# Attention 1 of a two-attention kernel: scores one item ahead, output weights converted later, a new order at the passage to attention 2

## The reference

```python
# attention 1: 32 heads of 128, 8 key/value heads, ALiBi-like bias, causal
qkv = h @ w_qkv                                   # h: x times a gate
scores = einsum('bqhd,bkhd->bhgqk', q, k) * 128 ** -0.5
attn = softmax(scores - slopes * sqrt(distance))  # -inf above the diagonal
x = x + einsum('bhgqk,bkhd->bqhgd', attn, v).reshape(B, S, 4096) @ w_o
# attention 2: q and k RMS-normed and rotated; 512 cached keys and values from pages, then 128 own ones
scores = einsum('bqhd,bhkd->bhqk', q, k_all) / sqrt(128)
y = einsum('bhqk,bhkd->bhqd', softmax(masked scores), v_all) @ Wo.T
# then a LayerNorm and two 8-bit-quantised linear layers; x = x + result
```

## Time and profile before

| | us |
|---|---|
| median of three runs | 2095.12 (2093.95 to 2095.36) |
| the profiled execution | 2088.9 |
| its span, first to last instruction | 2087.1 |
| TensorE busy | 2011.7 |
| VectorE, ScalarE, GpSimd busy | 1534.5, 1331.6, 825.6 |
| mean granted TensorE clock | 0.988 of full |

### The profile page before, as it was taken

One profiled execution on the slowest core, in us unless ns is written; L12 is line 12 of the kernel. 1 busy time (PEld: TensorE's weight loads), 2 busy tenths in 40 slices (PEclk: granted clock), 3 DMA queues, 4 the chain that ended last, 5 costly groups with the idle time before them and its releaser, 6 DMA issues.

```text
span 2087.1 us, 35849 instructions
## 1 busy us (share of the span) xinstructions
PE 2011.7 (96%) x12456; PEld 1701.8 (82%) x12456; DVE 1534.5 (74%) x3381; ACT 1331.6 (64%) x3810; POOL 825.6 (40%) x812
## 2 busy tenths in 40 slices
PE   6999999999999999989999999999999999999985
PEld 5777777888888888868888888888888888888873
DVE  5677765556656555568887887888878878888887
ACT  3567773445544544457776776777767767777785
POOL 4100014100000000035666666666666666666773
PEclk9999999999999999999999999999999999999997
DMA  8011101101201110111121110111211111112000
GB/s 299 26 52 47 51 1 71 61 31 36 67 31 36 56 46 6 56 46 50 31 83 31 61 52 31 62 52 31 83 32 62 53 31 62 53 31 81 27 31 30
DMA packets 45010, 108.60 MB, mean 52 GB/s; under 512 B 15634, under 2 KB 21010, under 8 KB 40354
## 3 DMA queue, kind: packets, MB, share of 16 engines
q1 hardware_dynamic: 28450, 72.74, 10.1%
q0 software_dynamic: 16384, 33.59, 5.3%
HBM read 103.14 MB, written 3.15 MB: 51 GB/s over the span
## 4 chain that ended last, share of the span: by engine, by line
PE 87%; DVE 7%; ACT 4%; issue 1%; DMA 0%; POOLq 0%; POOL 0%; SPq 0%; DVEq 0%; ACTq 0%
PE PS L1640 10%; PE PS L1544 8%; PE PS L1652 8%; PE PS L1416 8%; PE PS L1472 7%; PE PS L1607 7%; PE PS L1625 6%; PE PS L1558 4%; PE PS L1429 4%; PE PS L1610 3%; PE PS L344 3%; PE PS L1459 2%; PE PS L1444 2%; PE PS L334 2%; PE PS L500 1%
## 5 line engine op out<-in xcount | busy, mean ns | idle before, releaser
L2453 POOL DMA_INDIRECT kcache<-in_kcache,rows x256 | 251.2, 981 | 545.2 <-DVE x_res L1789 474.6
L2461 POOL DMA_INDIRECT vcache<-in_vcache,rows x256 | 257.5, 1006 | 137.4 <-PE PS L1444 61.7
L1935 DVE CUSTOM_DVE_ANT_0 pr<-PS,ffn_weights,sm 128x640 f32<-128x640 f32 x256 | 225.4, 885 | 96.5 <-PE PS L1610 96.4
L1951 DVE TENSOR_TENSOR prT_lo<-PS,prT_hi 128x512 fp32r<-128x512 f32 x320 | 209.4, 686 | 36.0 <-ACT prT_hi L2316 23.6
L2305 ACT ACTIVATE pr<-pr,sm 128x640 f32<-128x640 f32 x256 | 212.5, 831 | 36.5 <-DVE sm L1935 36.1
L2316 ACT ACTIVATE prT_hi<-PS 128x512 fp32r<-128x512 f32 x320 | 178.6, 597 | 66.3 <-PE PS L1625 63.7
L1625 PE MATMUL PS<-consts,pr 128*128 128x128 f32 x1280 | 174.0, 273 | 3.3 <-issue 1.5
L1625 PEld LDWEIGHTS PS<-consts,pr 128*128 128x128 f32 x1280 | 149.7, 141 | 29.4 <-issue 3.2
L2467 POOL TENSOR_TENSOR vcached_lo<-vcache,vcached_hi 128x512 fp32r<-128x512 f32 x64 | 83.2, 1300 | 226.7 <-ACT vcached_hi L2288 226.7
L2180 ACT ACTIVATE pr<-pr,sm 128x128 f32<-128x128 f32 x256 | 99.7, 391 | 100.5 <-DVE sm L1779 100.5
L1607 PE MATMUL PS<-kT_lo,qT_hi 128*128 128x320 f32 x512 | 154.1, 309 | 0.0
(11 more groups left out here) (324 smaller groups left out, 6224.9 us busy)
## 6 DMA issues: line engine op xcount, KB each, us to landing
arena<-in_wqkv SPq DMA_DIRECT2D x16, 1536.0 KB, 6.5
arena<-in_wo SPq DMA_DIRECT2D x16, 1024.0 KB, 5.5
arena<-in_wcT SPq DMA_DIRECT2D x8, 1024.0 KB, 5.8
kcache<-in_kcache,rows POOLq DMA_INDIRECT x256
vcache<-in_vcache,rows POOLq DMA_INDIRECT x256
arena<-in_xT SPq DMA_DIRECT2D x8, 256.0 KB, 6.6
x_res<-in_x SPq DMA_DIRECT2D x1, 2048.0 KB, 14.8
ffn_weights<-in_alibi SPq DMA_DIRECT2D x2, 1024.0 KB, 7.1
```

Of the source, the lines that this page charges most:

```text
L1935: dve.tensor_tensor_reduce(pr2[:, h, :].rearrange("p (a n) -> p a n", a=2), PS[:, SCORE_BANK[h]:SCORE_BANK[h] + 2, 0:HALF], keymask[:, b, ...
L1951: dve.tensor_tensor(prT2[1][:, n % 3, :, :].rearrange("p h n -> p (h n)"), bank(4 + n % 2), prT2[0][:, n % 3, :, :].rearrange("p h n -> p ...
L2453: pool.indirect_dma_start(out=kcache[:, c, :], out_offset=None, in_=T["kcache"], in_offset=bass.IndirectOffsetOnAxis(ap=rows[:, g, b, c:c ...
L2461: pool.indirect_dma_start(out=vcache[:, c, :], out_offset=None, in_=T["vcache"], in_offset=bass.IndirectOffsetOnAxis(ap=rows[:, g, b, c:c ...
```

## The change

In the TensorE's `step1`, the scores of items from 7 on move from the head of their item to the item before, between `turn_probs1` and `weigh1`; `turn_k1` of the same item goes ahead of the first head part. The VectorE's `softmax_max1(i + 1)` goes to the end of its step i, ahead of the sum's low part. In a group's first item three of the four low parts of output weights go behind the sum's low part, and `project_out1` waits for each quarter of those weights instead of all. In items 59 to 63 the work for attention 2 is distributed in another way over the items on all engines. On the GpSimd `load_values(0)` is split in two.

```diff
+        AHEAD = range(7, ITEMS)
             def project_out1(i):
-                pe.wait_ge(a1_wol, GH * (i // B + 1))
...
                 for h in range(GH):
+                    if i % B == 0 or h == 0:
+                        pe.wait_ge(a1_wol, GH * (i // B) + h + 1 if i % B == 0 else GH * (i // B + 1))
...
             def step1(i):                      # TensorE
-                scores1(i)
+                if i not in AHEAD:
+                    scores1(i)
                 if i + 1 < ITEMS:
                     if i > GH:
                         project_kv1(i + 1)
                 else:
                     project_kv(0)
-                    turn_cached_k(0)
+                if i == ITEMS - 1:
+                    turn_q(0)
                 if i >= FROM_X:
                     turn_x(i - FROM_X)
                 project_out1(i - 1)
+                if i + 1 in AHEAD:
+                    turn_k1(i + 1)
...
-                elif i == ITEMS - 3:
-                    project_q(0, (0,))
                 turn_probs1(i)
-                if i + 1 < ITEMS:
+                if i + 1 in AHEAD:
+                    scores1(i + 1)
+                elif i + 1 < ITEMS:
                     turn_k1(i + 1)
...
+                elif i == ITEMS - 5:
+                    project_q(0, (0, 1))
+                elif i == ITEMS - 4:
+                    project_q(0, (2,))
                 elif i == ITEMS - 3:
-                    project_q(0, (1, 2))
+                    project_q(0, (3,))
                 elif i == ITEMS - 2:
-                    turn_q(0)
+                    turn_cached_k(0)
                 elif i == ITEMS - 1:
-                    turn_k(0)
+                    project_q(1, (0, 1, 2))
                 weigh1(i)
...
                 elif i == ITEMS - 1:
-                    project_q(1)
+                    turn_k(0)
+                    project_q(1, (3,))
...
             def step1(i):                      # VectorE
                 g, b = group_of(i)
-                softmax_max1(i)
+                if i not in AHEAD:
+                    softmax_max1(i)
...
+                if i == ITEMS - 5:
+                    lo_of_weights(0, 0)
+                    lo_of_weights(0, 1)
+                if i == ITEMS - 4:
+                    lo_of_weights(0, 2)
+                if i == ITEMS - 3:
+                    lo_of_weights(0, 3)
+                if i == ITEMS - 2:
+                    dve.wait_ge(s_rope, 1)
+                    spread_q(0)
+                normalise1(i)
+                if b == B - 2 and g < G - 1:
+                    lo_of_weights1(g + 1, GH)
                 if i >= FROM_X:
                     lo_of_x(i - FROM_X)
+                if i == ITEMS - 2:
+                    lo_of_weights(0, KT)
+                    lo_of_probs1(i)
+                    add1(i - 1)
                     lo_of_v1(i + 1)
+                    join_q(0)
+                elif i == ITEMS - 1:
+                    lo_of_cached_k(0)
+                    lo_of_own_v(0)
                     rotate_k(0)
+                    lo_of_probs1(i)
                     norm_k(0)
+                    add1(i - 1)
                     lo_of_q(0)
                     lo_of_own_k(0)
+                else:
+                    add1(i - 1)
+                    lo_of_v1(i + 1)
+                    lo_of_probs1(i)
                 if b < GH and 0 < g < G - 1:
                     lo_of_weights1(g + 1, b)
+                if i + 1 == ITEMS - 1:
+                    add_alibi1(i + 1)
+                    lo_of_o1(i)
+                    row_max1(i + 1)
+                elif i + 1 in AHEAD:
+                    softmax_max1(i + 1)
+                    if b == 0 and g > 0:
+                        lo_of_out_weights1(g, 0)
+                    lo_of_o1(i)
+                else:
+                    lo_of_o1(i)
                 if b == 0 and g > 0:
-                    for h in range(GH):
+                    for h in range(1, GH):
                         lo_of_out_weights1(g, h)
-                lo_of_o1(i)
...
             def step(i):                       # VectorE, attention 2
-                if i == 0:
-                    add1(ITEMS - 1)
...
                 lo_of_probs(i, 0)
                 lo_of_probs(i, 1)
+                if i == 0:
+                    add1(ITEMS - 1)
...
             def step1(i):                      # ScalarE
+                if i == ITEMS - 5:
+                    hi_of_weights(0, 0)
+                    hi_of_weights(0, 1)
+                if i == ITEMS - 4:
+                    hi_of_weights(0, 2)
+                if i == ITEMS - 3:
+                    hi_of_weights(0, 3)
+                if i == ITEMS - 1:
+                    k_squares(0)
+                exps1(i)
                 if i >= FROM_X:
                     hi_of_x(i - FROM_X)
-                exps1(i)
                 if i + 1 < ITEMS:
                     kv_copies1(i + 1)
+                if b == B - 2 and g < G - 1:
+                    hi_of_weights1(g + 1, GH)
...
+                    hi_of_q(0)
+                if i + 1 in AHEAD:
+                    kT_copy1(i + 1)
                 hi_of_probs1(i)
...
             pool.wait_ge(a1_sc, ITEMS)
-            load_values(0)
+            load_values(0, (0, 1))
             factors(0)
+            load_values(0, (2, 3))
             load_keys(1)
```

More of the change, by code:

```diff
@@ L1771, in lo_of_out_weights1, with add_alibi1 @@
                                   ALU.subtract).then_inc(a1_wol, 1)
-            def softmax_max1(i):
+            def add_alibi1(i):
                 g = i // B
@@ L1813, in step1 @@
                 if i >= FROM_X:
                     lo_of_x(i - FROM_X)
-                normalise1(i)
-                add1(i - 1)
-                if i + 1 < ITEMS:
+                if i == ITEMS - 2:
+                    lo_of_weights(0, KT)
+                    lo_of_probs1(i)
+                    add1(i - 1)
                     lo_of_v1(i + 1)
-                if i == ITEMS - 4:
-                    for t in range(KT):
-                        lo_of_weights(0, t)
-                if i == ITEMS - 2:
-                    dve.wait_ge(s_rope, 1)
-                    rotate_q(0)
-                    lo_of_weights(0, KT)
@@ L1835, in step1 @@
                 if b < GH and 0 < g < G - 1:
                     lo_of_weights1(g + 1, b)
-                if b == B - 2 and g < G - 1:
-                    lo_of_weights1(g + 1, GH)
+                if i + 1 == ITEMS - 1:
[9 more added lines that the diff above has]
+                    lo_of_o1(i)
@@ L1878, in lo_of_out_weights, with spread_q @@
                                   ALU.subtract).then_inc(a2_wol, 1)
-            def rotate_q(n):
+            def spread_q(n):
                 g, b = group_of(n)
@@ L1893, in rotate_q @@
                 dve.tensor_tensor(qk2[:, 0:GH * P], qk2[:, 0:GH * P], swapped2[:, 0:GH * P], ALU.add).then_inc(a2_qr, 1)
+            def rotate_q(n):
+                spread_q(n)
+                join_q(n)
             def rotate_k(n):
@@ L2455, in load_keys, with load_values @@
                                             ).then_inc(a2_kg, 16)
-            def load_values(n):
+            def load_values(n, cs=range(CHUNKS)):
                 g, b = group_of(n)
                 wait(pool, a2_vcl, n)
-                for c in range(CHUNKS):
+                for c in cs:
                     pool.indirect_dma_start(out=vcache[:, c, :], out_offset=None, in_=T["vcache"],
```

24 lines of the change are left out of this document (8 added, 16 removed).

## The result

The changed kernel took 2064.92 us (median of 4 runs, 2061.49 to 2066.06) beside 2094.53 us (4 runs, 2092.81 to 2095.36) of the kernel before: ratio 0.9864, 95% interval 0.9848 to 0.9880, so some 28.5 us less. The forecast was 2067.3 in a range of 2061 to 2080. The profiled execution took 2064.42 us with a span of 2062.6 (before 2088.9 and 2087.1).

The account below looks back on a forecast made before the run. TensorE bounds attention 1's body, its busy count hiding a weight-load wait; the passage is loose. 9.5 + 2.6 + 14.2 + 1.5 = 27.8 us takes 2088.9 to 2061.1; with 6.2 to the median, 2067.3, range 2061 to 2080.

Parts of the forecast that it names:

- The ledger: Prediction's timed layout of one new item: cover before `weigh1` grows from 1.91 to 2.7 us against 1.96 needed.
- A: Attention 1, items 6 to 58: scores one item ahead remove `weigh1`'s 0.18 us wait, 9.5 us in 53 items.
- B: Items 8, 16 ... 48: output weights behind the sum's low part remove six stalls of 0.43, 2.6 us; bounds 0 and 2.6.
- C: Passage to attention 2, items 59 to 63: new order takes 42.4 instead of 56.6 us, gain 14.2, no clock fall.
- D: Attention 2, item 0: `add1(63)` moved behind two low parts frees the queries' read, 1.5 us; bounds 0 and 1.9.
- The two waits: Item 0 of attention 2: TensorE's 0.8 us for the third query product and 0.7 behind it were to go.
- The first: Rival: only counted idle time goes, the 0.18 is a change of data type, A gives nothing; 2076.8 us, 12%.
- the second: Rival: the passage keeps its chain through clock fall or longer VectorE queue; gain about 20 us, 2075 us, 22%.
- The third: Rival: earlier `softmax_max1` makes the sum late for `project_out1`, 0.9 us in 52 items, 47 us; 2126 us, 3%.

Follow-up runs that it names:

- head_cover: Kernel before with only the last three matmuls of each query head moved ahead of `weigh1`, from item 6 on; 2082.63 us, ratio 0.9954.
- old_weights: Changed kernel with all four low parts of output weights back ahead of the sum's low part in each group's first item; 2065.46 us, ratio 0.9876.
- before_again: Kernel before, unchanged, run beside itself for a second profile; 2085.00 us, ratio 0.9992.
- bunched: Changed kernel with the four query weight conversions back in item 60 and the whole first query product in item 61; 2059.44 us, ratio 0.9861.
- experiment 3: For D: changed kernel with `add1(63)` again ahead of `rotate_q(1)`; 2057.72 us (one run), item 0 of attention 2 19.66 us against 17.61 and 17.67.

## Why the prediction was right

**What bounds it.** Right. The decisive step was to take the wait of `weigh1`'s weight load as time, though the TensorE counted as 99.8% busy there. `head_cover` shows it by itself. The ledger had only 0.05 us of cover missing (1.91 against 1.96) and took the price, 0.18, from the chain. The trace of the kernel before shows how the one becomes the other:

```profile
494.38 0.40 PE L1416 MATMUL PS<-xT_lo,w_qkv_hi 128*128 128x512 f32 x1
494.69 0.50 PE L1459 MATMUL PS<-prT_hi,vown_hi 128*128 128x512 f32 x1
495.03 0.39 PE L1459 MATMUL PS<-prT_lo,vown_hi 128*128 128x512 f32 x1
```

The first matmul of `weigh1` starts 0.31 us after the one before it and the second 0.34 after the first, where 0.23 is the pace: 0.08 for being late and 0.11 more behind it.

The sentence on busy time in the Trainium skill (Trainium Kernel Development and Optimization, Performance Expectations) is borne out in numbers: 445.00 of 445.00 us count as busy in the changed body, 448.92 of 450.00 in the old, and yet an item takes 9.10 instead of 9.27 us.

**A, 9.5 forecast.** `old_weights`, which has A without B, gains 9.3 us to the end of head 63 (518.52 - 510.13, and the 0.89 of item 59's scores), 8.4 against the second profile of the kernel before. The low part is ready 0.8 us ahead of `weigh1` (610.86 and 611.64), as the ledger had it (2.7 of cover against 1.96). The lone key transposition costs 0.11 and so takes nothing. Not seen by me: in this order of the VectorE, A depends on the earlier place of the doubled weight conversion, 2.1 us.

**B, 2.6 forecast, 3.4 measured.** The mis-sized term is the stall, 0.43 in the old order and 0.57 in the new. The bound of 2.6 was therefore no upper bound: a stall read from the old order says what it costs there, not what it would cost with the other edits in place.

**C, 14.2 forecast, 14.6 measured** in the first pair. Period by period, from the end of head 63: 5.14 to the scores of item 60, where I had 5.3; 8.69 for 8.45; 7.97 for 7.75; 7.99 for 7.95; 12.07 for 12.95. Two errors nearly cancel. The first: a block of scores stands with 1.10 us in the chain here, not 0.89, four times, as in item 61:

```profile
873.56 1.11 PE PS L1445 x8
874.67 0.70 PE PS L1553 x3
```

The matmuls of the scores are no slower. What is new is a wait ahead of them, for the ScalarE's copy of the transposed key (rows of item 61, ScalarE and weight loads):

```profile
873.16 0.28 ACT L2218 ACTIVATE pr<-PS 128x128 f32<-128x128 f32 x1 [1.58 <-PE PS L1437]
873.50 0.97 PEld L1445 LDWEIGHTS PS<-pr,qT_odd 128*128 128x128 f32 x8 [0.18 <-issue]
```

The profile names no releaser for these 0.18 us, but the times do: in items 60 to 63 the first weight load of the scores starts 0.07 us after this copy has ended, each time; in the body the copy ends 0.55 us ahead of it, since three matmuls of a head (0.70 us) stand between the key's transposition and those of the probabilities. With the heads done, nothing stands there. The ledger of the body counted this margin, that of the passage allowed for the copy in item 62 alone. This is the term that C lacked: 0.2 us each in items 60, 61 and 63. The waits for the sum's low part in items 60 to 62, some 0.3 each, it had.

The second error goes the other way. By the net lengths of its blocks the work of item 63 is 11.15 us (an estimate: scores 0.89, keys and values 1.39, output 2.80, query product 2.80, two `weigh1` 1.40 and 1.87 of transposes), so its 12.95 held 1.8 of waits, of which the prediction names 0.8; measured are 0.9.

No fall of the clock, as forecast; the experiments add that the old passage's own length varies by 3 to 4 us with it, so that C was worth 14.6 us in the first pair and some 3 more beside `before_again`. The rule of the Trainium skill (TensorE: Matmul & The Clock Gate, Part 1), that an idle array is taken to 1.2 GHz and that activity brings it back, agrees with `bunched`: 1.00 in the gap, 0.50 behind it, 1.00 again in item 62. The prediction's other remark, that a gap can pass without a fall, holds too: the gap of 3.0 us in item 60 did so in two profiles of four.

**D, 1.5 forecast, 0.8 in the pair, 2.0 in experiment 3.** The two waits went, as said. What came in their place is the late first row maximum, which no row of the kernel before could show, since the VectorE was idle for 2.5 us there.

**Rivals.** The first fell with `head_cover`, the second with the passage. The third's mechanism exists and its price was wrong: its slack is 1.5 us in an ordinary item, not 0.5. I had put the end of the maximum at 3.6 and the start of the sum's low part at 3.95 and then counted only the slack behind that part; the time in front of it, 0.35 in the ledger and 0.97 in the profile, is also free. A maximum 1.44 us late costs 19 us, not 47, and by my estimate the gain is used up at about 1.6 us (19 us at 1.44, then 35 more for the next 0.72, one run).

**The time.** 2067.3 against 2064.92. The sum, 27.8, is 0.3 from what the profiles show up to item 1 of attention 2, and 1 to 4 us below what the three ratios give (28.5, 31.6 and 30.6 us). That the sum is so near is partly luck: B came out 0.8 above its forecast and D 0.7 below, C 0.4 above with two errors of its own. Of the profiled execution the prediction said 2061.1, and it took 2064.42, 3.3 more, since attention 2 gave back what nothing in the sum allows for. The distance of 6.2 us between profile and median that I left in place was no property of the kernel: for the changed one it is 0.5. So the median came 2.4 us below its forecast, and the profile 3.3 above.

## What to carry to other kernels

Where an engine looks full, look for waits of its weight loads and compare the net length of the same block at two places of the program; the cheapest test is to move matmuls that exist already into the hole. An in-order engine's slack is the idle time in front of the urgent instruction plus the one behind it, and it has to be read for each kind of item, since one extra conversion can use it up. A weight load that is late by 0.08 us cost 0.19 here, so short waits count. Gaps of 1.3 to 3 us on the TensorE cost more than themselves in some executions, so an order without gaps also makes the stretch steadier. And when a block of matmuls goes away, look at what it covered: the key's copy stood behind the heads' matmuls unseen until the heads were done.

## What the runs showed of the hardware

- The granted clock is not the same for the same gap: behind the 3.04 us of item 60 it was 1.00 in two profiles and 0.50 in two, behind the 1.30 us of item 59 it was 0.50 in one of four. From the scores of item 59 to those of attention 2 the four took 56.6 to 60.5 us, the longer the lower their mean clock (0.94 to 0.86).
- A weight load that waits costs more than its own lateness: 0.19 us for 0.08 at `weigh1` in the kernel before.
- The first row maximum of attention 2 behind the new passage begins 1.3 us after the scores on one chip and 2.9 us on two others, and the seventh items of attention 2 take 17.2 or 18.0 us in the same division. Between kernels this is up to 8 us of difference that belongs to neither, so that such kernels have to be compared on one chip, side by side.
